# When the split blocks store their second half, and how GpSimd's transfers lie in the first attention

## The reference, cut to what matters

```python
# layer 0: softmax attention over the normalised input, and a switch of 8 experts (top 1)
q, k, v = (einsum('bnhd,ed->bnhe', data, W) for W in (Wq, Wk, Wv))
attn = softmax(einsum('bqhd,bkhd->bhqk', q, k) / d ** 0.5)
x = x + (attn @ v) @ Wo.T + bo + experts_top1(xn)
# layer 1: causal, with a relative bias of 32 buckets for each head, and 8 experts (top 2)
att = einsum('bhtd,bhsd->bhts', q, k) / sqrt(D) + rel_bias
att = softmax(where(causal, att, -inf))
x = x + (att @ v) @ W_proj + b_proj + experts_top2(xn)
```

## Time and profile before

| | us |
|---|---|
| median of 3 runs | 1080.37 |
| lowest, highest | 1078.07, 1094.94 |
| the profiled execution | 1078.96 |
| its span, first to last instruction | 1076.9 |
| front block of layer 0 | 0 to 50.7 |
| attention of layer 0 | 50.7 to about 430 |
| front block of layer 1 | 497 to 533 |
| attention of layer 1 | 533 to about 800 |

### The profile page before, as it was taken

How to read it: one execution, slowest core, us unless ns; L and a number is a source line. 1 busy time by engine, 2 the same in 40 slices (tenths; PEclk the granted TensorE clock), 3 DMA queues, 4 the chain that set the end, 5 groups by cost and what they waited for, 6 DMA issues and landing times. The chain is left out here.

```text
span 1076.9 us, 22105 instructions
## 1 busy us (share of the span) xinstructions
PE 911.0 (85%) x8503; PEld 461.5 (43%) x8503; DVE 821.2 (76%) x1629; ACT 608.8 (57%) x1270; POOL 181.9 (17%) x216
## 2 busy tenths in 40 slices
PE   3479999998999988893599999999998977775698
PEld 2312222222222222892345445555445755554368
DVE  6799999997799970555598787777853669798687
ACT  2308888886688867451327677776753336232462
POOL 3102030513401200450200010003000010022122
PEclk9759999998899988896769999999978988888799
DMA  2842323534237210101861543333201000000001
GB/s 59 280 99 48 80 43 79 115 61 102 78 78 213 78 18 13 48 31 47 274 146 37 132 99 84 85 90 84 47 7 33 2 1 1 1 1 0 3 6 35
DMA packets 62224, 73.70 MB, mean 68 GB/s; under 512 B 20744, under 2 KB 46465, under 8 KB 62106
## 3 DMA queue, kind: packets, MB, share of 16 engines
q1 hardware_dynamic: 52730, 53.66, 20.0%
q0 software_dynamic: 8672, 18.15, 6.7%
q10 hardware_dynamic: 720, 0.50, 0.1%
HBM read 44.59 MB, written 18.16 MB: 58 GB/s over the span
## 5 line engine op out<-in xcount | busy, mean ns | idle before, releaser
L909 ACT ACTIVATE a_probs<-a_ebank 128x512 f32<-128x512 f32 (+3 forms) x896 | 436.3, 554 | 194.2 <-PE a_ebank L790 99.9
L951 DVE TENSOR_REDUCE a_negmax<-a_mbank 128x1 f32<-128x1024 f32 (+4 forms) x640 | 488.4, 818 | 74.5 <-PE a_mbank L769 34.4
L761 PE MATMUL a_mbank<-a_moving,a_still 48*128 48x512 bf16 (+4 forms) x1280 | 266.2, 380 | 28.2 <-DVE a_negmax L916 17.8
L790 PE MATMUL a_ebank<-b_moving,b_still 50*128 50x512 bf16 (+4 forms) x1280 | 270.7, 367 | 21.7 <-ACT a_probs L909 15.6
L813 PE MATMUL a_acc<-a_probs,a_slot_v 128*32 128x512 f32 (+3 forms) x1792 | 227.6, 581 | 1.1 <-ACT a_probs L909 1.1
L790 PEld LDWEIGHTS a_ebank<-b_moving,b_still 58*64 58x64 bf16 (+1 forms) x1280 | 84.8, 102 | 260.1 <-ACT a_probs L909 199.1
L761 PEld LDWEIGHTS a_mbank<-a_moving,a_still 56*64 56x64 bf16 (+1 forms) x1280 | 69.3, 104 | 97.1 <-DVE a_negmax L951 64.0
L799 PE MATMUL a_ebank<-a_bias_b,anti 64*64 64x176 bf16 (+4 forms) x1728 | 86.8, 229 | 0.0
L799 PEld LDWEIGHTS a_ebank<-a_bias_b,anti 64*64 64x64 bf16 x1728 | 68.6, 109 | 8.9 <-issue 0.4
L769 PE MATMUL a_mbank<-bias_a,anti 64*64 64x176 bf16 (+3 forms) x576 | 64.9, 240 | 0.0
L813 PEld LDWEIGHTS a_acc<-a_probs,a_slot_v 128*32 128x32 f32 x1792 | 35.8, 109 | 52.8 <-issue 40.7
(11 more groups left out here) (359 smaller groups left out, 1115.2 us busy)
## 6 DMA issues: line engine op xcount, KB each, us to landing
a_slot_v<-vo SPq DMA_DIRECT2D x16, 512.0 KB, 5.3
b_moving<-stack SPq DMA_DIRECT2D x64, 96.0 KB, 3.5
b_still<-stack SPq DMA_DIRECT2D x32, 192.0 KB, 4.0
a_still<-stack SPq DMA_DIRECT2D x58, 96.0 KB
a_moving<-stack SPq DMA_DIRECT2D x58, 96.0 KB
expert<-in_expert_rows POOLq DMA_DIRECT2D x8, 578.0 KB
stack<-expert SPq DMA_DIRECT2D x8, 384.0 KB, 3.7
stack<-parts SPq DMA_DIRECT2D x8, 384.0 KB, 4.1
```

What stands on the lines that cost most here:

```text
L761: last = nc.tensor.matmul(mbank[COLS * c:COLS * (c + 1), bank, lo - left:hi - left], S.a_still[rows, q % 2, pr, at[c]:at[c] + COLS], S.a_m ...
L790: last = nc.tensor.matmul(ebank[COLS * c:COLS * (c + 1), s % NE, lo:512], S.b_still[rows, buf, pr, at:at + COLS], S.b_moving[rows, buf, h, ...
L909: nc.scalar.activation(probs[:, g % 2, j, lows[g]:512], ebank[:, s % NE, lows[g]:512], ACT.Exp).then_inc(p_full, 1)
L951: nc.vector.tensor_reduce(to[:, at:at + 1], mbank[:, (index - 1) % NM, 0:right - left], AX.X, ALU.max, negate=True).then_inc(m_empty, 1)
```

## The change

It does five things. (1) In layer 0's front block GpSimd clears rows 1 to 5 of `vo` as its very first instruction, and DVE rows 6 to 8 with three memsets of 1024 columns. (2) In both layers the front block stores only chunks 0 and 1, and of these first the 32 partitions that quad 0 needs (`QUAD0`), 12 DMAs; when they have landed, SP loads the first pass's second pair and GpSimd the first; neither waits for the landing inside the block. (3) The other 96 partitions (`OTHERS`, 12 DMAs) are stored after that: in layer 0 still in the front block, in layer 1 in the attention, between `load_b(0, 0)` and `load_b(1, 1)`; SP waits for their landing before `load_b(1, 1)`. (4) Chunks 2 and 3 are stored during quads 1 and 2, one side before and one after the turn; SP waits for them at quad 3, before it loads quad 4. (5) GpSimd's transfers of the first attention are placed by first-pass units: one indirect DMA per two units (units 4, 6 ... 18) in quads 4 and 5, one expert in quad 5, three at units 4, 10 and 16 of quad 6, four at units 4, 8, 12 and 16 of quad 7, and the sorted rows in two loads.

```diff
 def front_phase, gpsimd
             if first:
+                nc.gpsimd.memset(S.vo[:, 1:6, :], 0.0).then_inc(v_cleared, 1)
                 pool.wait_ge(weights_loaded, 32)
...
-                nc.gpsimd.memset(S.vo[:, 1:, :], 0.0).then_inc(v_filled, 1)
-                pool.wait_ge(v_filled, 1)
+                pool.wait_ge(v_cleared, 4)
             nc.gpsimd.memset(v[:, :, :, :, HD:HD + 1], 1.0).then_inc(v_filled, 1)
-            for k in range(CHUNKS // BATCH):
-                pool.wait_ge(stored[k], 96)
-            for pr in range(2 if first else 1):
-                for jj in range(2):
-                    for dma in load_first_pass(pool, S, not first, 0, pr, jj):
-                        dma.then_inc(operands_loaded if first else S.first_loaded, 16)
-            if first:
-                pool.wait_ge(operands_loaded, 8 * 16)
+            pool.wait_ge(S.first_stored, 2 * 96)
+            for jj in range(2):
+                for dma in load_first_pass(pool, S, not first, 0, 0, jj):
+                    dma.then_inc(S.first_loaded[0], 16)
 def front_phase, vector
+                for q in range(6, NQUAD + 1):
+                    nc.vector.memset(S.vo[:, q, :], 0.0).then_inc(v_cleared, 1)
 def front_phase, sync
-            for k in range(CHUNKS):
...
+            for k in range(CHUNKS // BATCH):
                 for side in range(2):
                     sp.wait_ge(split, 2 * k + side + 1)
+                    for dma in store_split(sp, S, k, side, QUAD0):
+                        dma.then_inc(S.first_stored, 16)
-            for k in range(CHUNKS if first else CHUNKS // BATCH):
-                sp.wait_ge(stored[k], 96)
+            sp.wait_ge(S.first_stored, 2 * 96)
+            for jj in range(2):
+                for dma in load_first_pass(sp, S, not first, 0, 1, jj):
+                    dma.then_inc(S.first_loaded[1], 16)
             if first:
+                for k in range(CHUNKS // BATCH):
+                    for side in range(2):
+                        for dma in store_split(sp, S, k, side, OTHERS):
+                            dma.then_inc(S.stored[k], 16)
                 sp.wait_ge(ones_loaded, 32)
+def store_split(eng, S, k, side, rows):
+    W = CT * P
+    to = S.stack[k // 2, rows, :, side, k % 2 * W:(k % 2 + 1) * W]
+    dmas = []
+    for at, n in ((0, 3), (3, 2), (5, 1)):
+        part = 0 if side else (0, 3, 5).index(at)
+        src = S.parts[rows, k, side, part:part + (n if side else 1), :]
+        dmas.append(eng.dma_start(to[:, at:at + n, :], src.to_broadcast([rows.stop - rows.start, n, W])))
+    return dmas
 def attention_phase, sync
-            if causal:
-                load_a(0, 1)
             load_b(0, 0)
+            for k in range(CHUNKS // BATCH):
+                if causal:
+                    store_rest(k, 0, OTHERS)
+                    store_rest(k, 1, OTHERS)
+            for k in range(CHUNKS // BATCH):
+                sp.wait_ge(S.stored[k], 96)
             load_b(1, 1)
...
-                if q == 2 and causal:
-                    for stored in S.stored[CHUNKS // BATCH:]:
-                        sp.wait_ge(stored, 96)
+                if q in (1, 2):
+                    store_rest(q + 1, 0, ALL_ROWS)
+                if q == BQ - 1:
+                    for k in range(CHUNKS // BATCH, CHUNKS):
+                        sp.wait_ge(S.stored[k], 96)
...
                 for pr in range(2):
                     load_a(q + 1, pr)
+                if q in (1, 2):
+                    store_rest(q + 1, 1, ALL_ROWS)
 def attention_phase, gpsimd (reach(q, use) waits for m_full >= q * USES + use)
-                pool.wait_ge(m_full, USES + 5)
+                reach(1, 10)
                 load_late(slice(0, third))
-                pool.wait_ge(m_full, 2 * USES + 5)
+                reach(2, 10)
                 load_late(slice(third, 2 * third))
                 gather(0)
-                pool.wait_ge(m_full, 3 * USES + 10)
+                reach(3, 4)
                 load_late(slice(2 * third, None))
                 convert_masks()
                 add_bias()
                 gather(1)
-                pool.wait_ge(m_full, 4 * USES + 10)
+                reach(3, 24)
                 pool.dma_start(S.sorted_dram, S.empty_rows).then_inc(rows_cleared, 16)
-                sort_rows(range(NT // 2))
+                sort_rows(4)
                 gather(2)
-                pool.wait_ge(m_full, 5 * USES + 10)
-                load_experts(range(2))
-                sort_rows(range(NT // 2, NT))
+                sort_rows(5)
+                for k in range(CHUNKS // BATCH, CHUNKS):
+                    pool.wait_ge(S.stored[k], 96)
+                reach(5, 22)
+                load_expert(0)
                 gather(3)
-                pool.wait_ge(m_full, 6 * USES + 10)
-                load_experts(range(2, 5))
+                for i in range(3):
+                    reach(6, 4 + 6 * i)
+                    load_expert(1 + i)
+                reach(6, 23)
                 pool.wait_ge(rows_sorted, 16 * NT)
-                pool.dma_start(S.sorted[:], ...)
+                load_sorted(0, BT)
                 gather(4)
                 divide()
-                pool.wait_ge(m_full, 7 * USES + 10)
-                load_experts(range(5, EXPERTS))
+                for i in range(4):
+                    reach(7, 4 + 4 * i)
+                    load_expert(4 + i)
+                reach(7, 21)
+                load_sorted(BT, NB)
```

73 lines of the change are left out of this document (39 added, 34 removed).

## The result

The changed kernel takes 1071.82 us (median of 20 runs, 1063.89 to 1086.72) where the kernel before, on the same chip, takes 1082.94 (20 runs, 1071.13 to 1102.2). Within 2%, then, as forecast; 12.5 less was forecast. The profiled execution took 1070.29 us (span 1068.5, mean granted clock 0.908), against 1078.96 (1076.9, 0.900).

The account below looks back on a forecast made before the run. With TensorE busy 85% and VectorE 76%, no average decides; stages' own losses count. Terms -6.2, -8.7 and +2.4 sum to -12.5: 1066.5 us on the profiled execution, stated as 1067.9 for the median, range 1060 to 1077.

Parts of the forecast that it names:

- Layer 0's front, -6.2: Layer 0's front block: split memset and moved stores start the attention 6.2 us sooner, range -6.4 to -4.3.
- Rival D: Layer 0's front: DVE's memsets wait for GpSimd's, so the front's gain shrinks to -1.5; 1072.0 us, chance 0.07.
- The 5.6: Layer 0's front: 5.6 us go from DVE's first normalising instruction, 5.92 less 0.35.
- the 0.6 for the stores' landing: Layer 0's block end: 0.6 us more goes, as the old end also waited for stores to land.
- The spread, -9.7 and +1 against it: First attention: spacing GpSimd's indirect DMAs regains 80% of 12.1 us, -9.7; moved clearing and expert loads cost +1, bounds 0 and +4.
- The clearing of the sorted rows: First attention: 11.8 us of waiting for its landing moves to quad 3's unit 24, among quad 4's loads; within the +1.
- Layer 1's block end, -4.5: Layer 1's front block ends with GpSimd's and SP's last loads at 527.5 instead of 531.97: -4.5 us.
- Layer 1's queue, +6.9: Layer 1's attention start: stores in SP's queue delay the first rows, +7.3 us, with an estimated 0.4 back.
- A: First attention: the bursts are not the cause or hurt as much when spread; the term becomes +1, 1077.6 us, chance 0.16.
- B: Layer 1's queue costs nothing and the first attention recovers all; -20.3, 1060.1 us, chance 0.12.
- C: First attention: each indirect DMA following another's landing stalls by itself, 1.55 us each; +9.9, 1090.3 us, chance 0.05.
- the seven periods "near 41": First attention: sign that all seven periods between row groups take near 41 us; one near 47 would support A.

Follow-up runs that it names:

- experiment 1: Changed kernel with GpSimd again clearing all eight rows of the value store at once, after the weights, and VectorE none; ratio 0.9935 to the kernel before.
- experiment 2: Changed kernel with the sixteen indirect DMAs again as two bursts of eight, from unit 10 of quads 4 and 5; ratio 0.9992 to the kernel before.
- experiment 11: The changed kernel itself run again, without an edit; 1071.71 us, ratio 0.9884 to the kernel before.
- Experiment 5: Changed kernel with GpSimd's plain loads of the first attention moved by a few units, away from the rows of maxima; ratio 0.9998 to the kernel before.
- Experiment 3: Changed kernel with SyncE loading the first pass's pair 0 in layer 1's block and GpSimd loading pair 1 in the attention; ratio 0.9772 to the kernel before.
- experiment 4: Changed kernel with layer 1's first rows of maxima issued ahead of the wait for the twelve stores and load_b(1, 1); ratio 0.9808 to the kernel before.
- experiment 6: Changed kernel with layer 1's twelve stores of the other quads back in its block, behind the first pass's loads; ratio 0.9999 to the kernel before.
- experiment 10: Changed kernel with the sixteen indirect DMAs replaced by plain ones in two bursts of eight, sorting left out; one run, 1085.19 us beside 1094.35.

## Why the prediction was right, and the terms that were off

**Layer 0's front, -6.2: right (-5.97), in its parts too.** DVE's memsets took 0.91, near the 0.87 chosen between the ends, and the first normalising instruction starts 0.16 later than before (7.65, 7.49), where 0 was taken. Rival D falls: they ran beside GpSimd's. By the Trainium skill (SBUF — State Buffer, section "Who interferes with whom") a memset is not among the VectorE forms that take the shared port; the trace agrees, and the 5919 ns instruction of experiment 1 is of a form that can. The 5.6 is 5.3 at the end of DVE's chain, and the 0.6 for the stores' landing is 0.7.

**The spread, -9.7 and +1 against it: right in sum (-9.15), both terms too small.** The whole burst loss went, 12.1 and not 80% of it; of it experiment 2 brings 11.7 back by its two quads, and 8.5 to 9.8 by the whole stretch. Against it stood 3.2 of collisions in quad 5, and 3.3 more in quad 7 that the stretch of the table does not hold (+6.5 in all, above my upper bound of 4). So the sum of -8.7 was hit in part by luck: each term was too small, by 2.4 and 2.2, and the +3.2 is this execution's, 1.0 in experiment 11. I had priced a collision as PE's wait alone; where the clock falls behind the wait, that costs up to as much again, and where it holds the wait is the whole price (1.59 us of it cost 1.0 in experiment 11). The clearing of the sorted rows, which I also named, cost nothing: quad 3 takes 40.86. Experiment 5 shows the cause by moving the loads.

**Layer 1's block end, -4.5: wrong, and the one real error.** "Then GpSimd's six loads and SP's six end at 527.5, and with them the block": the issues did end 3.5 us after the landing (3.3 forecast), but the block waits for GpSimd's transfers to land, 4.9 us after the last issue instead of 1.1. Experiment 3 shows it. A second error hid a part of the first: the first rows landed 2.4 us after the fourth split (503.88 to 506.31), where 4.6 was forecast (519.63 to 524.2). From the split to the attention the term is -2.6. Eight profiles with this block have 98.6 to 100.6 us from the first load of sums to the attention, against 102.1 before, so with what the expert stage adds the term is about -2.2. The rule on the 16 ports that I weighed against this part (the Trainium skill, Advanced Engine Details and Errata, DMA Bandwidth Details) would have made 0.3 of difference, and no run here tells it apart.

**Layer 1's queue, +6.9: right in mechanism, and in sum (+7.05) with luck.** Its signs came: rows at T + 23.5, PE's wait 6.4. But the scores were only 5.7 later than before and not 7.2; the rest is PE's half clock behind its wait, which the sum did not hold. SP's queue and not the transfers bound it (experiment 4), and what is next behind them is the loads of quad 1, at once and for the same 6.4 us. So layer 1 is +5 (+5.5 in this pair) and not +2.4, at the upper bound; by experiment 6 it would be 5 better had the change left it alone.

**What nothing forecast: the clock in the attentions' ends.** In the profiled pair the first attention's end, less the 3.3 lost in quad 7, is 5.0 shorter at a mean clock of 0.98 against 0.91 over the stretch, and the second's is 1.9 longer (35.6, 33.7); the last 1.0 of the +2.9 lies behind it and was not followed up. Between executions of like kernels it is up to 13. It is part of the noise on both sides, and it is why single totals hid stages that moved by 3 to 6 us.

**Rivals.** A (the bursts not the cause) falls by experiment 2, B (layer 1 free) by the trace after, where the stretch is 7.05 longer, D by the memsets' rows. C (each indirect DMA stalls by itself) falls by the trace after: sixteen of them in quads 4 and 5, and quad 4 at 40.86. The signs named ahead held, except for the seven periods "near 41", of which quad 5's was 44.1, and the scores at 27.5 instead of about 29.

**What stays open.** Why a burst of indirect transfers holds up other engines, and only after 5 us, is not shown; it needs the close spacing (experiment 2 against the changed kernel), and either the indirect form or a burst of over 4.3 us (experiment 10). When the clock falls behind a wait of 1.3 to 1.7 us and when it does not is open too. And on the chip of the second group, where the kernel before took 1069.97 us, the three kernels nearest to the changed one stood at 1.000, 1.000 and 0.998: the changed kernel itself was not timed there, and its gain may be smaller on such a chip.

## What to carry to other kernels

When an early end is gained by moving work out of a block, list what the block's end still waits for (here GpSimd's transfers in flight) and what the moved work is now queued ahead of; the same twelve stores were free in a layer whose next rows come late and cost 5 us in the other. Price a stall of TensorE as a range: one of 1.73 us cost 1.2 where the granted clock held and 3.2 where it fell. Move big loads by a few units away from the small transfers that TensorE waits for, and judge such edits by the stage's length in the profile before the total.

## What the runs showed that I had not expected

- Eight indirect DMAs 1.3 us apart cost 5.5 to 6.2 us; the same eight 2.4 us apart nothing (quad 4); eight plain ones of the same bytes 0.54 us apart nothing.
- A block's end with six GpSimd transfers just issued took 4.9 us instead of 1.1 (1.8 with none).
- Twelve stores of 96 partitions took 8.0 to 9.2 us to issue, of 64 partitions 8.87, of 32 partitions 6.8 to 6.9.
- With 0.55 us of work in 4, PE's granted clock fell from 1.00 to 0.50 (1.2 GHz) and stayed there for the rest of the stage, some 25 us, although PE was then busy nearly all the time (experiment 4); in experiments 3 and 6, with 0.56 us of work in the same 4, it was back at 1.00 some 10 us after its fall.
